# Counting windows of a graph kernel: 128-column one-hots on ScalarE, a packed table word, counts spread anew, bias additions to X later

## The reference

```python
xn = _layernorm(x, axis=-1)
x = x + _L0_gnn_ref(xn, edge_index, edge_type_3, W1, q1, k1, b1, W2, q2, k2, b2) \
      + _L0_mix_ref(xn[None], W_qkv, b_qkv, W_out, b_out)[0]
x = x + _L0_ffn_ref(_layernorm(x, axis=-1)[None], weight_t, bias)[0]
# mix: q, k, v = split(xn @ W_qkv + b_qkv); qf, kf = phi(q), phi(k); kv = kf^T v; z = sum(kf)
#      y = (qf @ kv) / max(qf @ z, 1e-6); return y @ W_out + b_out       phi(t) = t + 1 if t > 0 else exp(t)
# gnn: per edge alpha = leaky_relu(q[type, dst] + k[type, src]), softmax over the edges of a dst, weighted sum of x W[type]
```

## Time and profile before

| | us |
|---|---|
| median of three runs (lowest, highest) | 2082.26 (2079.66, 2085.53) |
| the profiled execution | 2083.53 |
| its span | 2081.8 |
| PE busy | 1764.4 (85%) |
| DVE busy | 1372.2 (66%) |
| ACT busy | 781.1 (38%) |
| POOL busy | 289.8 (14%) |

### The profile page before, as it was taken

One profiled execution on the slowest core, in us unless ns is written; L12 is line 12 of the kernel. 1 busy time (PEld: TensorE's weight loads), 2 busy tenths in 40 slices (PEclk: granted clock), 3 DMA queues, 4 the chain that ended last, 5 costly groups with the idle time before them and its releaser, 6 DMA issues.

```text
span 2081.8 us, 39709 instructions
## 1 busy us (share of the span) xinstructions
PE 1764.4 (85%) x10571; PEld 1225.2 (59%) x10572; DVE 1372.2 (66%) x2626; ACT 781.1 (38%) x1044; POOL 289.8 (14%) x290
## 2 busy tenths in 40 slices
PE   2588777998999959994799999999599889999976
PEld 2244435666445635562599999998455445555544
DVE  6766566455574129998388888887227627777776
ACT  2122011122122025552487878785312113333342
POOL 2500000000011000110000000000011103333344
PEclk9899989887877989996899999999699999999998
DMA  4111010322111753332510030402245624111022
GB/s 159 49 41 39 19 42 32 86 63 82 54 60 35 281 143 127 119 110 87 170 50 25 28 122 25 125 25 80 90 140 173 205 91 167 45 45 45 9 99 74
DMA packets 123652, 180.13 MB, mean 87 GB/s; under 512 B 12677, under 2 KB 96526, under 8 KB 122810
## 3 DMA queue, kind: packets, MB, share of 16 engines
q1 hardware_dynamic: 123578, 179.16, 26.5%
HBM read 121.29 MB, written 57.84 MB: 86 GB/s over the span
## 4 chain that ended last, share of the span: by engine, by line
PE 61%; DVE 12%; issue 11%; DVEq 5%; DMA 5%; ACT 3%; SPq 1%; POOL 1%; ACTq 0%; POOLq 0%
PE ps L1844 18%; PE ps L1902 6%; PE ps L1901 6%; PE ps L1637 5%; PE ps L1638 5%; PE ps L1639 5%; PE ps L1651 4%; PE ps L1720 2%; DVE tt_junk L1384 2%; PE ps L1699 2%; DVE oh_p L1262 2%; DVEq L1260 2%; DMA xr_d<-ev 1%; DVE oh_q L1260 1%; PE ps L1772 1%
## 5 line engine op out<-in xcount | busy, mean ns | idle before, releaser
L1844 PE MATMUL ps<-xrh,pf 128*128 (+1 forms) x2400 | 406.7, 333 | 30.3 <-DVE pf L1468 24.4
L1844 PEld LDWEIGHTS ps<-xrh,pf 128*128 128x128 f32 x2400 | 402.7, 194 | 34.3 <-issue 33.2
L1637 PE MATMUL ps<-w_hi,xt_hi 128*128 128x384 f16 x960 | 331.3, 345 | 82.0 <-issue 34.1
L1260 DVE TENSOR_SCALAR oh_q<-pat,codeT,neg_w 125x630 uint16 x440 | 223.3, 508 | 177.4 <-issue 112.4
L1638 PE MATMUL ps<-w_lo,xt_hi 128*128 128x384 f16 x960 | 331.0, 345 | 0.0
L1639 PE MATMUL ps<-w_hi,xt_lo 128*128 128x384 f16 x960 | 330.2, 344 | 0.0
L1651 PE MATMUL ps<-oh_q,oh_p 125*128 x880 | 185.7, 348 | 54.1 <-DVE oh_p L1262 47.5
L1901 PE MATMUL ps<-x,ph 128*128 (+1 forms) x600 | 196.5, 327 | 19.3 <-POOL pl L858 19.3
L1468 DVE SCALAR_TENSOR_TENSOR pf<-vb,CT 128x1260 f32<-128x1260 f32 x120 | 175.6, 1468 | 54.4 <-PE ps L1844 54.4
L1464 DVE SCALAR_TENSOR_TENSOR vb<-vb,tb 128x1260 f32<-128x1260 f32 x120 | 174.6, 1468 | 45.8 <-ACT vb L1048 44.7
L788 POOL TENSOR_TENSOR w_lo<-wst,w_hi 128x2304 f16<-128x2304 f32 x20 | 92.5, 4628 | 788.9 <-ACT w_hi L878 760.4
(11 more groups left out here) (216 smaller groups left out, 2260.4 us busy)
## 6 DMA issues: line engine op xcount, KB each, us to landing
qbc<-tq_d SPq DMA_DIRECT2D x12, 1260.0 KB, 5.9
wst<-in_L_gnn_W SPq DMA_DIRECT2D x12, 1152.0 KB, 6.7
xr_d<-ev SPq DMA_DIRECT2D x60, 192.0 KB, 1.9
xrh<-xr_d SPq DMA_DIRECT2D x4, 2880.0 KB, 15.7
x_d<-ev SPq DMA_DIRECT2D x60, 192.0 KB, 2.2
x<-x_d SPq DMA_DIRECT2D x3, 3840.0 KB, 13.7
mb_d<-mb SPq DMA_DIRECT2D x30, 310.1 KB
mb<-mb_d SPq DMA_DIRECT2D x30, 310.1 KB
```

Of the source, the lines that this page charges most:

```text
L1260: dve.tensor_scalar(oh_q[0:ET, ds(slot + u, 1), :].rearrange("p o n -> p (o n)"), pat[0:ET, :], codeT[0:ET, ds(t + u, 1)], neg_w[0:ET, ds( ...
L1637: pe.matmul(ps[:, bank, 0:CW], a_hi, hi[:, k, :], start=(k == 0), stop=False)
L1844: mm = pe.matmul(out[b], pf[j][:, b * DB:b * DB + P], x, start=(first and b % 2 == 0), stop=False, skip_group_check=True)
```

## The change

1. ScalarE makes `oh_p`: for each pair two activations Abs(sloT - iota) of 128 columns into one half of a small double buffer (`gap_b`, `gap_c`), a wait for itself (`lo_abs`), and one Relu(1 - gap) over both, 256 columns. VectorE keeps `oh_q`. TensorE waits for both (`oh_rdy`, `lo_rdy`).
2. The table holds one word a window: first pair, count and running sum in 8, 8 and 16 bits. `window` loads it once and takes it apart by shifts and masks. TensorE reads all three fields too; ScalarE now reads the word as well.
3. The windows are spread anew: K 10, V 20, key-value sums 2 (new), Q 18 (12 before; three per block), behind Q 1, attention 9 (17 before). TensorE reads a window's word just ahead of the work that precedes its count. In V and in the key-value sums a count waits only for the copy of the window before the last.
4. On POOL the additions to X follow `w_lo` of chunks 2 to 4 and wait for the last V product (`g_done` 40).

```diff
-        def window(eng, w, with_tile0=True):
-            tile0 = eng.value_load(tabrow[0:1, ds(4 * w, 1)], min_val=0, max_val=NP - 3) if with_tile0 else None
-            count = eng.value_load(tabrow[0:1, ds(4 * w + 1, 1)], min_val=3, max_val=NP)
-            first = eng.value_load(tabrow[0:1, ds(4 * w + 2, 1)], min_val=0, max_val=NWN * NP)
+        def window(eng, w):
+            word = eng.value_load(tabrow[0:1, ds(w, 1)], min_val=0, max_val=(NWN * NP << 16) + (NP << 8) + NP)
+            tile0 = eng.snap(word & 255, min_val=0, max_val=NP - 3)
+            count = eng.snap((word >> 8) & 255, min_val=3, max_val=NP)
+            first = eng.snap(word >> 16, min_val=0, max_val=NWN * NP)
...
+        W_K, W_V, W_S, W_Q, W_R, W_A = 0, NB, 3 * NB, 3 * NB + 2, 3 * NB + 2 + 3 * K6, 3 * NB + 3 + 3 * K6
+        ATT_STEPS = (0, 3, 5, 8, 11, 13, 16, 19, 21)
...
+            for u in range(2):
+                store_window(sp, W_S + u, cb, u)
...
+            w_lo_part(2)
+            w_lo_part(3)
+            w_lo_part(4)
             pool.wait_ge(bias_in, 64)
+            pool.wait_ge(g_done, 4 * NB)
             pool.tensor_tensor(bsum[:, :], bsum[:, :], b2_bc0[:, :], ALU.add).then_inc(xb_done, 1)
...
                 pool.tensor_tensor(sub(X, i), sub(X, i), bsum[:, :], ALU.add).then_inc(xb_done, 1)
-            w_lo_part(2)
-            w_lo_part(3)
-            w_lo_part(4)
...
+            def low_hots(w, gap):
+                tile0, count, first = window(act, w)
+                with act.Fori(0, count) as jj:
...
+                    act.wait_ge(oh_free, first + jj + 1)
+                    act.wait_ge(lo_rdy, first + jj + 1)
+                    for u in range(2):
+                        last = act.activation(gap[0:ET, ds((first + jj) % 2, 1), u * P:(u + 1) * P].rearrange("p o n -> p (o n)"), iota_l[0:ET, :], ACT.Abs,
+                                              bias=sloT[0:ET, ds(t + u, 1)], scale=-1.0)
+                    last.then_inc(lo_abs, 1)
+                    act.wait_ge(lo_abs, first + jj + 1)
+                    act.activation(oh_p[0:ET, ds((first + jj) % (OHS // 2) * 2, 2), :].rearrange("p o n -> p (o n)"),
+                                   gap[0:ET, ds((first + jj) % 2, 1), :].rearrange("p o n -> p (o n)"),
+                                   ACT.Relu, bias=ones[0:ET, 0:1], scale=-1.0).then_inc(lo_rdy, 1)
...
                             window_out(w, 0, cb, 0, w)
+                            low_hots(w + 1, gap_b)
...
                     for u in range(2):
-                        window_out(W_V + 2 * m + u, 2 * u, cb, u, m + (W_V if u == 0 else 0))
+                        low_hots(W_V + 2 * m + u + 1, gap_b)
+                        window_out(W_V + 2 * m + u, 2 - 2 * u, cb, u, m + (W_V if u == 0 else 0))
                 w_hi_part(c + 4)
+            low_hots(W_S + 1, gap_b)
+            window_out(W_S, 2, cb, 0, 10 + W_V)
+            window_out(W_S + 1, 0, cb, 1, 10)
+            low_hots(W_Q, gap_b)
...
-                    window_out(W_Q + 2 * (3 * c + fb), 6, cc_, 0, 20 + 3 * c + fb)
+                    window_out(W_Q + 3 * q, 6, cc_, 0, 21 + 2 * q)
+                    low_hots(W_Q + 3 * q + 1, gap_c)
+                    window_out(W_Q + 3 * q + 1, 6, cc_, 1, 11 + q)
+                    low_hots(W_Q + 3 * q + 2, gap_c)
                     for g in range(NRG):
...
-                    window_out(W_Q + 2 * (3 * c + fb) + 1, 6, cc_, 1, 10 + 3 * c + fb)
+                    window_out(W_Q + 3 * q + 2, 6, cc_, 0, 22 + 2 * q)
+                    low_hots(W_Q + 3 * q + 3, gap_c)
...
                     y_hi_part(n - 1)
+                    if n + 1 in ATT_STEPS:
+                        low_hots(W_A + ATT_STEPS.index(n + 1), gap_c)
...
+            count_part(W_S + 1)
             dve.wait_ge(kvs_done, 2)
...
+            count_part(W_Q)
             dve.wait_ge(xb_done, NB + 1)
...
-                    if att_window(n) is not None and att_window(n) + 1 < NWN:
-                        count_part(att_window(n) + 1)
+                    if n + 2 in ATT_STEPS:
+                        count_part(W_A + ATT_STEPS.index(n + 2))
...
                     pe.wait_ge(oh_rdy, first + jj + 1)
+                    pe.wait_ge(lo_rdy, first + jj + 3)
...
-                pe.wait_ge(ct_ev, w + 1)
+                pe.wait_ge(ct_ev, w + 1 - out_first)
...
                 if p6 % 3 == 2:
                     last.then_inc(kvs_done, 1)
+                    count_window(W_S + p6 // 3, 2 - 2 * (p6 // 3), 1, window(pe, W_S + p6 // 3))
...
-                        if k == K6 // 2:
-                            count_window(wa, 6, *of_wa)
+                        if k in (2, 4):
+                            count_window(wa + k // 2 - 1, 6, 0, table)
+                        if k in (0, 2, 4):
+                            table = window(pe, wa + k // 2)
```

More of the change, by code:

```diff
@@ L65 @@
 M2_0 = 1
-KEEP = 9856
+KEEP = 9088
 WT_TILES = 2 * R * K6
@@ L185, in build @@
         tab = place("tab", [NTAB, 8], F32, 118112)
-        tabi = place("tabi", [NTAB, 4], I32, 118144)
+        tabi = place("tabi", [NTAB, 1], I32, 118144)
         ltri = place("ltri", [NTAB, NTAB], F32, 118176)
@@ L897, in window_out @@
                 act.activation(stage[u][:, :].rearrange("p (q n) -> p q n", q=2), ps[:, bank:bank + 2, 0:QH], ACT.Copy).then_inc(ct_ev, 1)
+            act.sem_inc(lo_rdy, 2)
+            def low_hots(w, gap):
+                tile0, count, first = window(act, w)
+                with act.Fori(0, count) as jj:
+                    t = nc.s_assert_within(2 * (tile0 + jj), 0, NT - 2, skip_runtime_bounds_check_because="tile0 + count <= NP for every window of the table")
+                    act.wait_ge(oh_free, first + jj + 1)
[8 more added lines that the diff above has]
+                                   ACT.Relu, bias=ones[0:ET, 0:1], scale=-1.0).then_inc(lo_rdy, 1)
+            act.wait_ge(tab_in, 16)
+            act.wait_ge(e_row, 7)
+            act.wait_ge(consts_done, 5)
+            low_hots(0, gap_b)
             for c in range(2):
@@ L935, in y_hi_part @@
                 act.activation(yt_hi[:, p6, g * RG:(g + 1) * RG], yv[n % 2][:, :], ACT.Copy).then_inc(y_hi, 1)
-            window_out(W_A - 1, 6, cc_, 0, 26)
+            window_out(W_R, 6, cc_, 0, 33)
+            low_hots(W_A, gap_c)
             def att_out(n):
-                if n >= 0 and att_window(n) is not None:
-                    k = att_window(n) - W_A
-                    window_out(W_A + k, 6, cc_, k % 2, k // 2 + (16 if k % 2 else 27))
+                if n in ATT_STEPS:
+                    k = ATT_STEPS.index(n)
+                    window_out(W_A + k, 6, cc_, (1 + k) % 2, k // 2 + (34 if k % 2 else 17))
             for n in range(K6 * NRG):
@@ L1642, in _, with count_window @@
             pe.wait_ge(tl_done, 2 * NB + 4)
-            def count_window(w, bank, count, first):
+            def count_window(w, bank, out_first, table):
+                _, count, first = table
                 def tile(jj, start, stop):
                     pe.wait_ge(oh_rdy, first + jj + 1)
+                    pe.wait_ge(lo_rdy, first + jj + 3)
                     for u in range(2):
@@ L1672, in _ @@
                         if counted:
-                            _, count, first = window(pe, w, False)
+                            table = window(pe, w)
                         pe.wait_ge(g_free, n + 1)
@@ L1676, in _ @@
                         if counted:
-                            count_window(w, 0 if c < 2 else 2 * j, count, first)
+                            count_window(w, 0 if c < 2 else 2 - 2 * j, c >= 2, table)
             pe.wait_ge(kv_out, 2 * NB + 2)
@@ L1728, in _ @@
                         wq_tile(t)
-                    count_window(wa + 1, 6, *of_wb)
-            of_w = window(pe, W_A - 1, False)[1:]
+                    count_window(wa + 2, 6, 0, table)
+            table = window(pe, W_R)
             for t in range(WT_TILES // 2, WT_TILES // 2 + 3):
                 wq_tile(t)
-            count_window(W_A - 1, 6, *of_w)
+            count_window(W_R, 6, 0, table)
             pe.wait_ge(q_out, 2 * 3 * NRG + 2)
@@ L1751, in _ @@
                     wq_tile(WT_TILES // 2 + 6 + n // 2)
-                if att_window(n) is not None:
-                    wa = att_window(n)
-                    count_window(wa, 6, *window(pe, wa, False)[1:])
+                if n in ATT_STEPS:
+                    wa = W_A + ATT_STEPS.index(n)
+                    count_window(wa, 6, 0, window(pe, wa))
             def node_columns(hi, lo, n):
```

53 lines of the change are left out of this document (29 added, 24 removed).

## The result

The changed kernel takes **2119.3 us** (median, 2114.9 to 2121.0) beside 2081.1 for the kernel before on the same chip: ratio 1.0177, 95% interval 1.0154 to 1.0199. It is slower by 38 us, and 15 above the upper end of the range. Its profiled execution took 2114.85 us, with a span of 2112.9 where before had 2081.8, so the stages have to account for +31.1.

The account below looks back on a forecast made before the run. VectorE was taken to bound K, V and attention, with TensorE close behind and Q mixed. Terms -14.5 - 1 - 10 + 15 + 17 - 22 = -15.5 us on 2083.53 gave 2068 us, range 2030 to 2104.

Parts of the forecast that it names:

- Q term: Q stage, 18 windows instead of 12: blocks of 26.5 us against 23.6, +17 us for six (+5 to +31).
- Attention's term: Attention, 9 windows instead of 17: a serial chain over ScalarE, 105 us against 127, -22 us (-38 to -10).
- pair A = 1.3: ScalarE's new one-hot pair, two Abs and a Relu: 1.3 us a pass, 1.1 to 1.6 possible.
- The start, -14.5: Kernel start: without POOL's additions beside the one-hots, first eviction at 73.6 instead of 88.1 us, -14.5 us.
- VectorE's pair, 1.0: VectorE's loop pass, losing two instructions and their register blocks: from 1.31 to about 1.0 us; window head 2.2 to 1.1.
- The slope of 137 us per us of pair: Whole kernel: a pair off by 0.1 us was to move the total by 14 us.
- K, -1: K stage, 10 windows: a turn of 10.1 us as before, -1 us; a turn over 11 would make it wrong.
- V, -10 (-18 to -3): V stage, 20 windows: TensorE becomes the bound at 7.6 us a window, -10 us; a count waiting for Relus would contradict it.
- Behind V, +15: Behind V: two windows between the key-value sums, +8, and TensorE held up by POOL's additions, 5; +15 us (+8 to +20).
- (1): Rival in K, Q and attention: ScalarE's pair takes 1.6 us, register work behind each wait; 2109 us, chance 0.20.
- (2): Rival in V, Q and attention: TensorE stays dense and its clock up; 2030 us, chance 0.25.
- (3): Rival on the moved additions: the stall only changes place, to V's end and Q, 10 more; 2078 us, chance 0.10.

Follow-up runs that it names:

- dve_hots: The changed kernel with oh_p made on VectorE again and none on ScalarE; packed word, moved additions and new spread kept: 2098.1 us, ratio 1.0064.
- q_two: dve_hots with two instead of three windows in each Q block, the six others counted in attention: 2067.9 us, ratio 0.9929.
- move_only: The kernel before with only the ten POOL additions to X moved behind the last V product: 2074.6 us, ratio 0.9971.
- new_spread_ahead: The changed kernel with ScalarE's Abs one pair ahead in four buffers of their own and a constant Relu bias: 2093.4 us, ratio 1.0043.
- act_pipelined: The changed kernel with ScalarE's next Abs written into the ring slot ahead of this pair's Relu, whose bias is a constant: 2125.4 us, ratio 1.0211.
- attention_uncounted: The changed kernel without the one-hots and counts of its last nine windows, so those counts are wrong: 2093.2 us, ratio 1.0054.
- word_move: The kernel before with the packed word and the moved additions; old spread, both one-hots on VectorE: 2058.6 us, ratio 0.9890.
- word_only: The kernel before with only the packed table word, one per window: 2068.6 us, ratio 0.9933.

## Why the prediction was wrong, step by step

By stages the +31.1 of the profiled executions is: start -15.6, K +3.7, V -5.2, behind V +15.2, Q +43.0, attention -11.2, the remainder +1.2. That is 46.6 over the forecast's -15.5. Q has 26 of it, attention 11, K and V 5 each. **The step that failed is the Q term**: a chain that priced a further window in a Q block at 2.9 us (17 / 6), where one measures 7.0 with VectorE's one-hots (42 / 6, dve_hots and q_two) and 7.2 with ScalarE's (43 / 6, before and after). Attention's term and the pair A = 1.3 were mis-sized beside it.

- **The start, -14.5: right.** First eviction at 72.53 (forecast 73.6), one-hots of 0.4. The hold of 5 by the additions, which the forecast booked behind V, falls within V in move_only.
- **VectorE's pair, 1.0: wrong, 1.28.** What was taken off for the two instructions, 0.31, is right: 0.30 from dve_hots to the changed kernel. What the term lacked is the packed word's price in every pass, 0.26, which was booked at a window's head alone. The head, 1.1, was 0.93.
- **ScalarE's pair, A = 1.3: wrong, 1.82.** It doesn't give the sign: at 1.23 (new_spread_ahead), and with no pair on ScalarE at all (dve_hots), the kernel is still slower than before. By the links of the forecast's chain: the two Abs 0.69 for 0.57, the wait behind them 0.19 for 0.05, and from the Relu's start to the next Abs 0.93 (87.69 to 88.62) for 0.65 to 0.7, which is half of the miss. An Abs takes 0.394, not 0.286, and the Relu 0.508, not 0.41. The row of 0.286 has no bias from memory. The two Abs need one, and the Relu was given one too: with a constant it takes 0.41 (243.63), so such a pointer costs 0.1. The Trainium skill (ScalarE: Activation LUTs, What ACT_TABLE_LOAD costs) states it: 280 ns + 0.833 ns an element with a pointer for the bias, 186 + 0.833 without, and back-to-back ones overlap by about 93. By its figures the Abs is an estimated 0.387 and the Relu an estimated 0.493, and the rows have 0.394 and 0.508; two Abs in 0.69 is twice 0.394 less that overlap. The prediction took the row to contradict the page's rule, but the row was of the other kind, and by the page's other figure it agrees (186 + 100 = 286).
- **The slope of 137 us per us of pair: wrong.** From 1.82 to 1.23 the changed kernel gains 26, a slope of 44, if all of the gain is put down to the price; act_pipelined, at 1.18, gains nothing, so it isn't the price alone. By that slope I estimate that at A = 1.3 the kernel would stand near 2096: the pair explains some 23 of the miss of 51, and 28 lies elsewhere.
- **K, -1: +3.7**, by the turn of 11.08 (over 11, one of the signs named); with A at 1.23 V starts at 171.0, 8.5 earlier, 5 better than the forecast.
- **V, -10 (-18 to -3): -5.2.** In its bounds. From 180 to 325 TensorE waits 12.8 us for its own queue at the products and 16.5 for one-hots, 9.9 of these for the Relus: the other sign named.
- **Behind V, +15: +15.2.** Right, and for the reasons given: POOL's additions run from 334.26, seven oh_q stretch over 12.50 us from 334.97, and TensorE waits 5.4 for oh_q from 334 to 367 (forecast 5), 1.81 of it at 346.04:

```profile
334.26 13.03 POOL L818 TENSOR_TENSOR X<-X,bsum 128x768 f32 x7 [0.26 <-POOL bsum L814]
...
334.97 12.50 DVE L1306 TENSOR_SCALAR oh_q<-pat,codeT,neg_w 125x630 uint16 x7
...
346.04 0.81 PE L1701 MATMUL ps<-oh_q,oh_p 125*128 x4 [1.81 <-DVE oh_q L1306]
```

- **Q, +17 (+5 to +31): +43, the largest error.** With A at 1.23 it is still +37.5. The block was forecast at 26.5 from a chain of copies, loads and pairs, with q's exponentials behind the third count, and measures 30.6, from a block's first projection to the next block's, the mean of five (before: 23.7; new_spread_ahead: 29.8; dve_hots: 29.6, with no pair on ScalarE). What the chain lacked: the third window's last pair needs a ring slot that comes free only in its own count, behind the weight products, and q_t stands behind that pair in VectorE's line; and a pair costs TensorE more than the 0.63 booked, 0.81 to 1.23 where it comes alone. q_two takes the third window out and has the 154 back.
- **Attention, -22 (-38 to -10): -11.2.** The forecast took the turns over ScalarE as the limit, and 2.75 for a window taken out (22 / 8). attention_uncounted shows the limit: 90 us of TensorE at half clock; in the changed kernel TensorE is busy 108 of 114 and waits 5.5 for one-hots. A window's price there, 2.75, was near what was measured by adding or removing some with one maker of one-hots (2.3 and 2.6; 3.1 from word_move to dve_hots), but with the change it saves 1.4 (11.2 / 8). Either is far from the 7.5 of 127 / 17, and nothing that the new spread does there could pay for 7.0 a window in Q.
- **The rivals.** (1), a pair of 1.6, had the right sign and nearly the number, 2109 against 2119, and the pair was longer still. Its mechanism is right for a part only: it puts all of the loss down to the pair, and without that pair the kernel stands at 2098. That the number came so near is in part luck. (2), TensorE dense and its clock up, did the opposite in attention. (3) held in part: move_only lost 5 at V's end, but no 10 beyond what was booked.
- The chance of slower, 0.23, came almost wholly from rival (1) (0.17). That the spread itself could be a loss, 40 us with VectorE's one-hots, was no rival: by the forecast's terms a window costs about the same in Q (2.9) and in attention (2.75), so moving it was nearly free.

**What stays open**: why TensorE's clock in attention is 0.65 in word_move and 0.82 in word_only, with the same 17 windows (128.3 and 117.3 us); the number of counts doesn't settle it. And how much of the spread's 40 is due to the words read ahead and the later wait for the copy: no run has them alone.

## What to carry to other kernels

Price a piece of filler work where it is put and where it is taken from, by adding and removing one: the same window cost 7.0 us in one stage and 2.3 in the other, where a chain written down beforehand had 2.9 and 2.75. When a value is packed to save loads, look at every pass of the loop that uses it, not only at its head: 1.3 us were saved there and 0.26 lost in each pass. Before work goes to an idle engine, ask what already stands in its line in each turn, and take the price from a row with the same kinds of operands. In a loop with a ring, put the wait for the slot at the instruction that needs it: the same pair, 1.2 us either way, cost 32 us more with the wait one instruction too early.

## What the runs showed of the hardware that was not expected

- A bias from memory makes an ACTIVATE 0.1 us longer: Relu of 256 columns 0.508 against 0.41.
- A dependent ACTIVATE starts 0.19 after the end of the one it waits for; 0.05 was assumed.
- Taking two of four instructions (0.25 each) out of a pass of VectorE's loop shortened it from 1.58 to 1.28; unpacking a table word by shifts and masks instead of three loads had lengthened it from 1.31 to 1.57, and shortened the window's head from 2.23 to 0.93.
- A stage in which TensorE is busy without a gap, 91 of 91 us, had a granted clock of 0.51; the K stage of new_spread_ahead, 91 of 103 busy, had 1.00. What it was busy with differs (kvd and spread products and weight products in f32 there, products in f16 here); which property decides isn't settled here.
